# Interleaved rows in the operand stacks of a decoder layer, and another order of the first loads and merges

## The reference

```
x = layernorm(x + self_attention(x))     # 16 heads of 32, q/k/v/o = x W^T + b + 0.5 (x B^T) A^T, rank 16
x = layernorm(x + cross_attention(x, c)) # channels attend: 16 heads of 16 channels over 512 features
x = layernorm(x + ffn(x))                # fp8-rounded operands, gelu(x Wg0) * (x Wg1), then Wo
```

## Time and profile before

| | |
|---|---|
| median of 3 runs | 2103.29 us |
| profiled execution, its own time | 2092.57 us |
| its span in the profile | 2090.7 us |
| TensorE matmul busy | 1969.1 us (94%) |
| VectorE, ScalarE, GpSimd busy | 1506.7, 1131.6, 979.2 us |
| mean granted TensorE clock | 0.953 |
| bytes by DMA | 220.56 MB, mean 105 GB/s |

### The profile page before, as it was taken

The page is one execution under the profiler, slowest core; times in us unless marked ns, Lnnn a source line. Parts: engine busy times, 40 slices in busy tenths (PEclk is TensorE's granted clock), DMA queues, the critical chain, the costliest instruction groups (busy, mean ns, idle before and its releaser), DMA issues.

```text
span 2090.7 us, 31790 instructions
## 1 busy us (share of the span) xinstructions
PE 1969.1 (94%) x11460; PEld 1054.3 (50%) x11460; DVE 1506.7 (72%) x2632; ACT 1131.6 (54%) x2117; POOL 979.2 (47%) x968
## 2 busy tenths in 40 slices
PE   7798999999999888999999999999999898999998
PEld 4576776767677643344444434433444333444443
DVE  3455666675656656788878878777888728999997
ACT  3233444444444424687878877777788673333331
POOL 3345555555455422244444434444344226666664
PEclk9899999999999868899999999999999889999999
DMA  5877787878777733465665565655565610111111
GB/s 151 136 140 137 144 154 124 171 126 146 138 132 141 144 56 64 96 105 128 122 124 106 105 112 108 108 100 106 98 113 93 166 40 11 51 41 41 41 61 41
DMA packets 149515, 220.56 MB, mean 105 GB/s; under 512 B 41463, under 2 KB 50167, under 8 KB 148615
## 3 DMA queue, kind: packets, MB, share of 16 engines
q1 hardware_dynamic: 139694, 216.95, 53.2%
q10 hardware_dynamic: 9664, 1.58, 0.6%
HBM read 83.95 MB, written 32.02 MB: 55 GB/s over the span
## 4 chain that ended last, share of the span: by engine, by line
PE 53%; DMA 20%; DVE 11%; POOL 6%; ACT 3%; issue 3%; SPq 3%; ACTq 0%; POOLq 0%; DVEq 0%
PE bank L1302 8%; PE bank L1596 8%; PE bank L1267 7%; PE bank L85 6%; DMA xa_sums<-xa_oc 5%; DMA sa_kst<-sa_part_kl 5%; PE bank L1572 4%; PE bank L86 4%; PE bank L87 4%; DMA inv<-xa_sums 4%; PE bank L1310 4%; PE bank L567 3%; DMA xa_den<-inv 3%; PE bank L622 2%; DVE xa_mneg L1345 2%
## 5 line engine op out<-in xcount | busy, mean ns | idle before, releaser
L1345 DVE TENSOR_REDUCE xa_mneg<-bank 128x1 f32<-128x512 f32 x1024 | 657.9, 681 | 200.8 <-PE bank L1310 197.4
L1167 ACT ACTIVATE xa_prob<-bank 128x512 f32<-128x512 f32 x1024 | 568.8, 600 | 211.7 <-PE bank L1302 202.5
L1310 PE MATMUL bank<-xa_kst,xa_qst 48*128 48x512 f32 x1024 | 414.6, 477 | 19.1 <-DVE xa_mneg L1345 14.5
L1302 PE MATMUL bank<-xa_qst,xa_kst 49*128 49x512 f32 x1024 | 400.9, 463 | 16.1 <-ACT xa_prob L1167 15.9
L458 ACT ACTIVATE sa_prob<-bank 128x512 f32<-128x512 f32 x256 | 152.4, 598 | 370.7 <-PE bank L622 370.1
L1302 PEld LDWEIGHTS bank<-xa_qst,xa_kst 49*128 49x128 f32 x1024 | 162.8, 190 | 333.1 <-ACT xa_prob L1167 259.0
L1267 PE MATMUL bank<-xa_prob,xa_v 128*32 128x512 f32 x2048 | 285.5, 631 | 0.0
L1504 POOL TENSOR_TENSOR ff_total<-ff_prod,ff_mag 128x512 f32<-128x512 bf16 x128 | 194.5, 1520 | 108.9 <-DVE ff_mag L1620 108.9
L692 DVE TENSOR_REDUCE sa_mneg<-bank 128x2 f32<-128x512 f32 x256 | 164.2, 682 | 51.6 <-PE bank L635 51.3
L1310 PEld LDWEIGHTS bank<-xa_kst,xa_qst 48*128 48x128 f32 x1024 | 165.1, 191 | 55.1 <-DVE xa_mneg L1345 39.0
L1548 ACT ACTIVATE ff_gelu<-bank 128x512 bf16<-128x512 f32 x128 | 75.5, 592 | 161.2 <-PE bank L1596 161.1
(11 more groups left out here) (191 smaller groups left out, 3729.9 us busy)
## 6 DMA issues: line engine op xcount, KB each, us to landing
xa_qst<-xa_part_q SPq DMA_DIRECT2D x192, 128.0 KB, 5.3
xa_kst<-xa_part_k SPq DMA_DIRECT2D x192, 128.0 KB, 6.4
sa_qst<-sa_part_qh SPq DMA_DIRECT2D x64, 256.0 KB, 6.3
sa_kst<-sa_part_kh SPq DMA_DIRECT2D x64, 256.0 KB, 8.8
xa_den<-inv SPq DMA_DIRECT2D x64, 256.0 KB
sa_xraw<-xT SPq DMA_DIRECT2D x8, 1024.0 KB, 8.2
sa_qst<-sa_part_ql SPq DMA_DIRECT2D x32, 256.0 KB, 6.0
sa_kst<-sa_part_kl SPq DMA_DIRECT2D x32, 256.0 KB, 10.2
```

The source lines that it names most:

```text
L1167: act.activation(prob[:, e % XPROBS, :], banks[eb[e]][:, :], ACT.Exp, scale=X_SCALE)\
L1302: pe.matmul(banks[eb[e]][:, :], kst[u % 3][rows_of, head // 2, t * P:(t + 1) * P], qst[u % 3][rows_of, head // 2, :], start=True, stop=Tru ...
L1310: pe.matmul(banks[mb[m]][:, :], qst[u % 3][rows_of, n // 8, t * P:(t + 1) * P], kst[u % 3][rows_of, n // 8, :], start=True, stop=True).the ...
L1345: dve.tensor_reduce(mneg[:, u % 2, column:column + 1], banks[mb[m]][:, :], AX.X, ALU.max, negate=True).then_inc(s_mfree, 1)
```

## The change

The rows of the stacks are interleaved. Dimension d of a head had its three terms in rows d, 32 + d and 64 + d; now in rows 3d, 3d + 1 and 3d + 2 (cross-attention: 48 rows, the same). Each transfer has the same bytes and the same source, and writes every third partition in place of 32 (or 16) consecutive ones. The sums over the rows have the same terms. Row 97 (49) stays.

The copies of the low-rank factors go to every second partition of their blocks of 32.

In the cross-attention the twelve stack transfers of a unit stood together in two slots (six at slot 20, six at slot 25); now one stands in each of the slots 20 to 31. In the self-attention the slots stay.

x is loaded in four pieces with a semaphore each, also later in the loop (slots 4 to 7 of the first unit of a pair, before all in slot 4). At the start W_q is loaded ahead of x, ScalarE takes the factors of v and q ahead of x, and the merges use other PSUM banks, with the last quarter of W_q's and all of W_k's waiting for the banks of v and q.

```diff
-    merge_bank = {"v": (3, 4, 5, 6), "q": (0, 1, 2, 7), "k": (3, 4, 5, 6), "o": (3, 4, 5, 6)}
+    merge_bank = {"v": (3, 4, 5, 6), "q": (1, 2, 7, 3), "k": (4, 5, 6, 7), "o": (3, 4, 5, 6)}
+    merges = [merge_bank[n][c] for n in MERGE for c in range(DC)]
...
-    def load_xraw(sp, wait, p):
-        low_done(wait, p - 1, range(DC))
-        sp.dma_start(xraw[:, :, :], a["xT"][p].rearrange("(c r) n -> r c n", r=P))\
-          .then_inc(s_xraw, 16)
+    def load_xraw(sp, wait, p, c):
+        low_done(wait, p - 1, [c])
+        sp.dma_start(xraw[:, c, :], a["xT"][p].rearrange("(c r) n -> r c n", r=P)[:, c, :])\
+          .then_inc(s_xraw[c], 16)
...
         load_w("v")
-        load_xraw(sp, wait, 0)
-        for n in "qko":
-            load_w(n)
+        load_w("q")
+        for c in range(DC):
+            load_xraw(sp, wait, 0, c)
+        load_w("k")
+        load_w("o")
...
-            for r, m in enumerate(parts):
-                sp.dma_start(dst[u % 3][r * SDH:(r + 1) * SDH].bitcast(F32),
-                             part[name + m][:, :].bitcast(F32)).then_inc(s_st[u % 3], 16)
+            sp.dma_start(dst[u % 3][r:3 * SDH:3].bitcast(F32),
+                         part[name + parts[r]][:, :].bitcast(F32)).then_inc(s_st[u % 3], 16)
...
-                act.dma_start(lora_raw[m][r * BLOCK:r * BLOCK + RANK], a["lora_" + m]).then_inc(s_lora, 16)
+                act.dma_start(lora_raw[m][r * BLOCK:(r + 1) * BLOCK:2], a["lora_" + m]).then_inc(s_lora, 16)
+        wait.wait_ge(s_lora, 16 * 6)
+        high_lora("v")
+        high_lora("q")
         for c in range(DC):
             high_x(act, wait, 0, c)
-        wait.wait_ge(s_lora, 16 * 6)
-        for n in "vqk":
-            high_lora(n)
+        high_lora("k")
         high_w("v")
...
-        for n in "vq":
-            for c in range(DC):
-                add_w(n, c)
-        for n in "vq":
-            for c in range(DC):
-                add_lora(n, c)
+        for n, c in [*(("v", c) for c in range(DC)), *(("q", c) for c in range(DC - 1))]:
+            add_w(n, c)
+        for n, c in [*(("v", c) for c in range(DC)), *(("q", c) for c in range(DC - 1))]:
+            add_lora(n, c)
+        add_w("q", DC - 1)
+        add_lora("q", DC - 1)
         merge("k")
...
-            for r, m in enumerate(order):
-                for side in range(2):
-                    row = side * 64 + r * XK
-                    sp.dma_start(dst[u % 3][row:row + XK].bitcast(F32),
-                                 part[name][side * 64:side * 64 + 64, m, :].bitcast(F32))\
-                      .then_inc(s_st[u % 3], 16)
+            rows_of = slice(side * 64 + r, side * 64 + XROWS, 3)
+            sp.dma_start(dst[u % 3][rows_of].bitcast(F32),
+                         part[name][side * 64:side * 64 + 64, order[r], :].bitcast(F32)).then_inc(s_st[u % 3], 16)
...
-            if (un := unit(slot, STACK_AT, 1)):
-                stack("q", un[0])
-            if (un := unit(slot, STACK_AT + 5, 1)):
-                stack("k", un[0])
+            for n, name in enumerate("qk"):
+                if (un := unit(slot, STACK_AT + 6 * n, 6)):
+                    stack(name, *un)
```

More of the change, by code:

```diff
@@ L161, in self_attention_phase @@
     S = 2 * SG
-    STACK_AT = {"q": S, "k": S + 1}
+    STACK_AT = {"q": (S, S, S), "k": (S + 1, S + 1, S + 1)}
     MAX_AT = 2 * S
@@ L302, in sync, with stack @@
         sp.dma_start(bob[:, :], a["bo"].partition_broadcast(P)).then_inc(s_bias, 16)
-        def stack(name, u):
+        def stack(name, u, r):
             wait.wait_ge(s_pl, 2 * u + "qk".index(name) + 1)
@@ L325, in sync @@
             for name in "qk":
-                if (un := unit(slot, STACK_AT[name], 1)):
-                    stack(name, un[0])
+                for r, at_slot in enumerate(STACK_AT[name]):
+                    if (un := unit(slot, at_slot, 1)):
+                        stack(name, un[0], r)
             i = round_tile(slot, 0)
@@ L349, in sync @@
                       .then_inc(s_xnat[n % 4], 16)
-            p, left = divmod(slot - 4, S * SG)
-            if left == 0 and p + 1 < PAIRS:
-                load_xraw(sp, wait, p + 1)
+            p, c = divmod(slot - 4, S * SG)
+            if 0 <= c < DC and p + 1 < PAIRS:
+                load_xraw(sp, wait, p + 1, c)
     def gpsimd(pool):
@@ L533, in project_chunk @@
                 bank_free(n)
-                if n < 3:
-                    wait.wait_ge(s_wlo, merged("q", n) + 1)
+                if n in merges and n < 3:
+                    wait.wait_ge(s_wlo, merges.index(n) + 1)
             if name == "v":
@@ L575, in add_w @@
             wait.wait_ge(s_w[n], 16)
-            if n == "k":
-                wait.wait_ge(s_wlo, merged("v", c) + 1)
-            elif n == "o":
-                wait.wait_ge(s_wlo, merged("k", c) + 1)
+            m = merged(n, c)
+            if merges[m] in merges[:m]:
+                wait.wait_ge(s_wlo, max(k for k in range(m) if merges[k] == merges[m]) + 1)
             pe.matmul(banks[merge_bank[n][c]][:, :], ident[:, :], wraw[n][:, c, :], start=True, stop=False)
@@ L975, in load_w, with stack @@
               .then_inc(s_w[n], 16)
-        def stack(name, u):
+        def stack(name, u, i):
+            r, side = divmod(i, 2)
             wait.wait_ge(s_pl, 2 * u + "qk".index(name) + 1)
```

16 lines of the change are left out of this document (9 added, 7 removed).

## The result

The changed kernel takes 2018.62 us (median of 4 runs, 2015.46 to 2021.17), the kernel before beside it 2103.51 us (2097.13 to 2109.44). The ratio is 0.9596, 95% interval 0.9565 to 0.9628: 85 us less. A second comparison, in another batch, gave 2019.73 against 2084.42 us, 0.9698 (0.9635 to 0.9762). The kernel before moves from batch to batch (medians 2084 to 2113 us in five batches); the changed one, in its two, did not. Medians are of all executions and ratios of the fast ones alone, so that a ratio can differ from the quotient of two medians. The forecast was 2060, the range 2036 to 2098: right in sign, and about half of the gain (43 of 85 us).

What follows compares the result with a forecast made beforehand. TensorE's matmuls were taken to bound both attention parts, with 36.9 us of self-attention waits hanging on stack transfers; terms summed to −43.5 us, 2092.6 to 2049, plus 10.7 gave 2060 us, range 2036 to 2098.

Steps and rivals of the forecast that it cites:

- the cross-attention's term: Cross-attention stretch, 790 to 1660 us: little to get with 24 us of idle time in 870; −5 us (+10 to −15).
- Transfer: Stack transfers: 256 KB written to every third of 96 partitions takes 1.1 us in place of 2.0 (lower end 0.65).
- First stacks: First unit's six stack transfers: the sixth lands at 56.8 in place of 62.2 us, TensorE's wait goes; −5 us (0 to −5.9).
- Self-attention with its clock: 62 to 700 us: most waits on stack transfers vanish, −25 us (0 to −31); less time at half clock, −11 (0 to −20).
- Start: Before the first projection: with W_q loaded ahead of x it begins near 27.5 in place of 32.30 us; −4.5 us (0 to −8).
- Give-back of +12: VectorE's bursts in the layer norms: TensorE, coming sooner, meets these waits more often; +12 us.
- The +10.7 us: Whole kernel: the median of the runs lies 10.7 us above the profiled execution; put on top of 2049, giving 2060 us.
- Handover: 700 to 790 us, before the cross-attention: first cross stacks land sooner and part of the slow clock goes; −5 us (0 to −10).
- Freed time that is not TensorE's: Rival: VectorE, ScalarE and the loop over the row of maxima take over half the gain; −22 us, 2081; chance 0.22.
- Transfer not faster: Rival: the source side or SBUF-to-SBUF copying limits stack transfers, only the start's gain is left; 2099 us; chance 0.11.
- The late last transfers of k: Rival, cross-attention: k's last two stack transfers, issued behind `inv`, land late in 32 units; 26 us slower, 2125; chance 0.07.
- a sign of being wrong: Cross-attention: waits for `xa_kst` of more than 5 us in all would show the forecast wrong.

Runs made afterwards that it cites:

- these rows alone: The kernel before with only the cross-attention stacks' rows interleaved, the twelve transfers still in two groups of six: 2052.6 us, ratio 0.9777.
- groups: The changed kernel with the twelve cross-attention stack transfers again in two groups of six, rows interleaved: 2003.81 us against the changed kernel's 2019.73 in that batch.

## Why the prediction was wrong, step by step

**What failed is the cross-attention's term**: "With 24 us of idle time in 870 there is little to get: −5." It was −24 in the profile, with the new wait at the last unit against it, and −38 in the profile of these rows alone (−43 by the medians). I took the sum of TensorE's idle time as a cap and looked only at its direct wait for a stack. Nor did I do for this stretch what I had done for the self-attention: a clock of 0.97 over 870 us is, by the same working, some 52 us at half speed and 26 us lost, and this term I had at nothing without a reason. What paced the units was a loop that passes through none of these: sums of exp to VectorE, reciprocals to DRAM, the spreading back, GpSimd's product, ScalarE's high part, and behind that in ScalarE's order the next exp. Three transfers of it, two of 8 KB and one of 256 KB, queue behind six or twelve of the stacks', and SP issues q's six stacks only when `inv` has landed, and the sums only behind these. The chain of waits of the kernel before, around the place of rows 10 and 11, shows it:

```profile
1198.43 1.97 DMA inv<-xa_sums
1200.41 0.65 SPq L1042
...
1201.15 0.63 SPq L989
...
1205.34 6.53 DMA xa_sums<-xa_oc
...
1212.17 7.20 DMA inv<-xa_sums
1219.38 3.58 DMA xa_den<-inv
...
1223.02 1.29 POOL xa_oc L1098
...
1225.70 0.39 ACT xa_oh L1206
...
1227.28 0.49 ACT xa_prob L1167
...
1227.91 0.46 PE bank L1302
```

8 KB take 6.5 and 7.2 us. I had `inv`'s issue at 1212.17 in the earlier trace rows and read it only as a thing that k's last transfers would have to wait for. In the changed kernel, SP issues `inv` at 1188.31 and what waits for its landing at 1190.26:

```profile
1188.31 0.55 SPq L1039 DMA_DIRECT2D inv<-xa_sums  x1
...
1190.26 0.66 SPq L1047 DMA_DIRECT2D xa_den<-inv  x1
```

That is at most 1.95 us. The loop then ends before it is wanted, and TensorE sets the pace. The idle time was no cap because a late unit costs in other ways as well, above all by the clock. Three stretches at half clock in the kernel before (10.2, 6.8 and 6.8 us, at 1244, 1360 and 1459) account for 11.9 us, the idle time for 562.90 − 553.56 = 9.3; 5.4 of the 26.7 us remain, in matmuls that the records show as busy. One of the three stretches:

```profile
1244.30:1254.50 10.20, 10.20 (x36) 3.44 (x36) 5.32 (x10) 5.55 (x11) 2.96 (x5) 0.50 0.15 54
```

The chain of the profile's summary had it: 20% DMA over the span, with the loop's three transfers at 5, 4 and 3%, some 250 us. I read the chain at one place of the self-attention and not for the cross-attention.

**The other terms.** *Transfer*: 1.1 us per 256 KB forecast, 1.13 measured, and 1.18 between the landings of the first unit (the first issued at 44.70 and landed 3.2 us later, the sixth landed at 53.78). That the middle of a scale of ratios hit it was luck; no row bore on it. The estimate worked from the Trainium skill (SBUF — State Buffer, "Door 1: The DMA port swizzle") was 1.35. Its rule, that 32 more is the same port, is borne out (every second row gains nothing); that two thirds of the bytes on the lower half would set the pace is not, and the measurement decides. "The trace agrees" was also too much: 32 partitions go at a third of the rate of 128 (127 and 382 GB/s), where eight of sixteen ports would give half. The four pieces of x land 4.3 us after their issue (median of the run; 12.9 us at the start, behind W_v and W_q), and cost nothing that the profile shows.

*First stacks*: −5 forecast. The first projection to the first maximum took 29.9 us before and takes 24.6 now, −5.3. *Self-attention with its clock*: −25 − 11 = −36 forecast for 62 to 700, −36.4 found, of which 22.9 is idle time of TensorE and 13.5 busy time. Both parts are of the size forecast; that the sum agrees to 0.4 us is luck, since this stretch took 670.3 to 674.6 us in the four executions with consecutive rows in both attentions, and 633.4 to 642.4 with the self-attention's rows interleaved. The waits for `raw` and the maxima's row are 5.1 us, though one of 1.2 and three of up to 2.4 us stayed, over the limit of 1 us that I had set. The clock of 62 to 700 is 0.98, as forecast. *Start*: −4.5 forecast, −3.1 in the profile, −7 by the runs; the first projection starts at 29.2 and not at 27 to 28. The merge of k, put at 1.5 us, took 5.0:

```profile
23.58 5.03 PE L584 MATMUL bank<-sa_wraw_k,ident 128*128 128x512 f32 x8
...
29.16 0.19 PEld L85 LDWEIGHTS bank<-sa_wvh,sa_xh 128*128 128x128 f32 x1
```

Half of that was at the 1.2 GHz level (the granted clock is 0.50 from 19.6 to 26.4), and its weight loads wait 0.6 and 0.8 us for VectorE's low parts of W_v and W_q. *Give-back of +12*: not there. VectorE's waits went from 25.7 to 26.6 us. Ending TensorE's other waits hardly lengthened these; the term had no row behind it. *The +10.7 us* between profiled execution and median belonged to the scatter of the kernel before; after, the two differ by 0.6 us. The give-back and this, together 22.7 us too much, are rather more of the miss than the 19 us that the cross-attention's term lacks in the profile. *Handover*: −5 forecast, not separated; the whole stretch from the first cross-attention maximum to unit 10 went from 318.1 to 316.2 us.

With −24 for the cross-attention and without the two additions, the working gives 2092.6 − 43.5 − 19 − 12 = 2018 us, as measured; but that takes −5 for a handover that was hardly there (2) and leaves out the 6.0 behind the last unit, so it is no proof of the terms.

**The rivals.** Freed time that is not TensorE's: wrong, units 10 to 30 have TensorE busy all the time. Transfer not faster: wrong. The late last transfers of k: their mechanism came once, in another shape. Not `inv` but the feed-forward weights stand ahead of the last one, at one unit and not at 32; it costs 8.4 us at its place. That is more than the 5 us of waits for `xa_kst` that I had named as a sign of being wrong. Spreading costs 16 us against groups in the one batch that had both. What taking the one wait away by moving the loads is worth stays open, since the stretch behind it varies by as much.

## What to carry to other kernels

Read the chain of waits for every stretch before capping a term by an engine's idle time, and count the clock in every stretch: an engine that is 97% busy can still be paced by a loop of transfers. When large transfers get faster, the small ones behind them in the queue can gain more (here from 7.2 to at most 1.95 us, where the large ones went from 6.4 to 2.9), so list what else lands through the same queue and who waits for it. Prove such a loop by cutting it and leaving the large transfers slow, and look at what else the cut sets free.

## What the runs showed of the hardware that I had not expected

The cost of a transfer from SBUF into 32 partitions depends on which these are, and not in proportion to their distance: 127, 129, 231 and 382 GB/s for every, every second, third and fourth partition. Alternating transfers between rows from 0 and rows from 64 gives nothing (127 GB/s). The same 32 consecutive partitions take 211 GB/s from DRAM, in pieces of 8 KB in place of 2, so 127 is no limit of the partitions written alone; what sets it stays open. Nor is it clear that turns never help: 128 KB into every third of 48 partitions of one side land 1.04 us apart, and in the kernel, with both sides in turn as source and as destination, 0.63 us apart.
